# A two-lane decoder kernel on one Trainium2 core: SyncE begins the shifted copies and the expert stores, the queries' norm moves into the exponential's scale, and the lanes' turns change

## What is computed

```python
x = LN(x + state_space(x))           # RMS norm, in-projection, causal convolution, selective scan over T, 16 states
x = LN(x + cross_attention0(x, ctx)) # 16 heads of 64, tanh gate
x = LN(x + experts(x))               # 8 experts, top 2, and one shared expert, FF 512
x = LN(x + window_attention(x))      # 16 heads of 8, rotary, window 128
x = LN(x + cross_attention1(x, ctx)) # 16 heads of 8
x = LN(x + local(x))                 # 2 layers, see below
```

```python
q, k = l2norm(q) * q_scale, l2norm(k) * k_scale
q, k = rotary_xpos(q, k)                       # a query sees its own block of 64 keys and the one before
attn = softmax(mask(8 * q @ k.T)); x = x + (attn @ v) @ wo
h = layernorm(shift(x)) * lg + lb; a, g = split(h @ w1 + b1); x = x + (a * gelu(g)) @ w2 + b2
```

## Time and profile before

| | us |
|---|---|
| median of 3 runs | 1565.3 |
| lowest and highest run | 1559.88, 1567.16 |
| span of the profiled execution, first to last instruction | 1544.1 |
| time of the profiled execution itself | not given |
| busy: PE, DVE, ACT, POOL | 1269.2, 1046.3, 808.2, 395.7 |
| mean granted TensorE clock (1 is full speed) | 0.911 |

### The profile page before, as it was taken

The page is one execution under the profiler, slowest core; times in us unless marked ns, Lnnn a source line. Parts: engine busy times, 40 slices in busy tenths (PEclk is TensorE's granted clock), DMA queues, the critical chain, the costliest instruction groups (busy, mean ns, idle before and its releaser), DMA issues. The chain is left out here.

```text
span 1544.1 us, 23279 instructions
## 1 busy us (share of the span) xinstructions
PE 1269.2 (82%) x8400; PEld 815.4 (53%) x8400; DVE 1046.3 (68%) x2162; ACT 808.2 (52%) x2180; POOL 395.7 (26%) x248
## 2 busy tenths in 40 slices
PE   5767878887998888789775888889689988988986
PEld 4412335884665556456531233579456654655663
DVE  4789976226887787378449998741378879746853
ACT  2466423453764556466627553336276636665663
POOL 0036633412000332032011665360400023202300
PEclk9789978997999989999987888989799999999997
DMA  8300001780000100001010000068400000000000
GB/s 298 123 0 1 0 1 54 254 268 19 2 1 1 35 21 15 1 15 28 2 28 0 1 0 1 1 201 263 130 1 2 1 1 22 22 1 14 22 8 14
DMA packets 42179, 72.21 MB, mean 47 GB/s; under 512 B 3793, under 2 KB 27473, under 8 KB 41810
## 3 DMA queue, kind: packets, MB, share of 16 engines
q1 hardware_dynamic: 28242, 56.30, 10.8%
q10 hardware_dynamic: 11776, 10.23, 2.6%
q0 software_dynamic: 2048, 4.20, 0.9%
HBM read 51.19 MB, written 13.24 MB: 42 GB/s over the span
## 5 line engine op out<-in xcount | busy, mean ns | idle before, releaser
L912 POOL TENSOR_TENSOR scratch<-scratch 128x1024 f32<-128x1024 f32 x64 | 149.7, 2353 | 140.4 <-DVE scratch L883 119.9
L634 POOL TENSOR_TENSOR small<-small,w_const 128x16 f32<-128x16 f32 x32 | 101.1, 3163 | 298.2 <-DVE small L1753 298.2
L731 PE MATMUL psum<-scratch,w_const 128*128 128x512 f32 x256 | 148.8, 713 | 18.5 <-POOL scratch L912 18.4
L883 DVE TENSOR_TENSOR_SCAN scratch<-psum,scratch 128x512 f32<-128x512 f32 x128 | 150.1, 1206 | 9.5 <-ACT psum L804 8.9
L634 POOL TENSOR_TENSOR rstd<-rstd,w_const 128x4 f32<-128x4 f32 x32 | 32.8, 1029 | 432.9 <-DVE rstd L596 430.3
L1706 ACT ACTIVATE scratch<-psum,mx 128x128 f32<-128x128 f32 x256 | 90.0, 376 | 72.7 <-DVE mx L1794 71.5
L804 ACT ACTIVATE psum<-scratch,a_neg 128x512 f32<-128x512 f32 x128 | 87.8, 690 | 61.2 <-DVE scratch L883 52.1
L1374 ACT ACTIVATE scratch<-psum,mx 128x256 f32<-128x256 f32 (+1 forms) x256 | 111.2, 465 | 10.0 <-DVE mx L1410 8.4
L720 PE MATMUL psum<-scratch,cb 96*128 96x512 bf16 x128 | 49.7, 428 | 60.6 <-DVE scratch L875 51.3
L1160 ACT ACTIVATE scratch<-psum,scratch 128x128 f32<-128x128 f32 x240 | 68.3, 368 | 54.7 <-PE psum L1101 54.6
L1541 PE MATMUL psum<-w_local,hT 128*128 128x512 f32 x192 | 91.2, 615 | 6.3 <-ACT hT L1523 5.1
(11 more groups left out here) (266 smaller groups left out, 3199.6 us busy)
## 6 DMA issues: line engine op xcount, KB each, us to landing
expert_weights<-in_expert_weights SPq DMA_DIRECT2D x61, 512.0 KB, 5.1
scratch<-scratch ACTq DMA_DIRECT2D x48, 128.0 KB, 2.3
folded_products<-expert_weights SPq DMA_DIRECT2D x8, 512.0 KB, 3.1
folded<-folded_products SPq DMA_DIRECT2D x8, 512.0 KB, 4.7
w_local<-in_local SPq DMA_DIRECT2D x1, 3122.0 KB
sorted_y<-scratch ACTq DMA_DIRECT2D x12, 256.0 KB, 5.6
scratch<-sorted_x SPq DMA_DIRECT2D x4, 704.0 KB, 6.7
scratch<-in_cross SPq DMA_DIRECT2D x1, 2624.5 KB, 12.9
```

The costliest lines, as they stand in the source:

```text
L634: t.eng.tensor_tensor(v, v, W("const", "neg_half").to_broadcast([P, v.shape[1]]), ALU.pow).then_inc(t.s[done], 1)
L731: ins = pe.matmul(sum_banks[c], ident, t.m.hC[:, 2 * ((n - 1) % 2) + c, :], start=(n == 1), stop=(n == NS))
L883: dve.tensor_tensor_scan(t.m.hs[:, n % 2, c, :], t.ps["dA"], t.m.dBu[n % 2][:, c, :], 0.0, ALU.mult, ALU.add)\
L912: t.eng.tensor_tensor(t.m.hC[:, 2 * (n % 2):2 * (n % 2) + 2, :], t.m.hs[:, n % 2], C, ALU.mult)\
```

## The change

1. **Copies and stores.** The pair of shifted copies and the expert stores are begun by SP, in `row_sync`, and no longer by ACT. SP's loop over the blocks runs four steps longer; the stores stand in it behind the same counts of `block_copied`. The copies wait on SP for `v_freed`.
2. **The queries' norm.** DVE multiplies only the keys by their inverse norm (512 columns instead of 1024). The queries' inverse norm becomes the scale of the exponential, read from SBUF for each head, and DVE multiplies the negative row maxima by it in an added product of 128x4, behind a wait for the maximum's own step.
3. **Masks.** For u = 0 the mask matmul is issued first and the wait for the turned queries' and keys' copies (`a_freed`) comes behind it, in a step of its own.
4. **The table.** All five lists are new. Changes of lane and steps: PE 511 to 732 turns, ACT 435 to 558, DVE 714 to 868, POOL 131 to 126, SP 27 to 68. A local layer has 78 steps on PE instead of 74.

The diff, with the lists cut to the first line of one:

```diff
@@ TURNS @@
 TURNS = {
     "pe": [
-        5, 21, 4, 3, 1, 10, 2, 5, 4, 4, 2, 1, 6, 2, 3, 3, 3, 3, 3, 3, 5, 3, 3, 3, 3, 3, 3, 3, 3, 5, 3, 3, 3, 3,
...
+        5, 34, 4, 1, 1, 4, 2, 3, 1, 1, 3, 1, 4, 1, 1, 1, 3, 3, 3, 3, 3, 3, 3, 3, 5, 2, 1, 1, 2, 2, 1, 1, 2, 3,
...
@@ -1139,13 +1155,6 @@
                 n = min(4, NBK - 4 * g) * P
                 act.activation(t.m.xsT[:, 4 * g * P:4 * g * P + n], t.a.take()[:, 0:n], ACT.Copy).then_inc(t.s["a_freed"], 1)
 
-            def store(g):
-                yield
-                n = min(4 * g + 4, NBK)
-                act.wait_ge(t.s["block_copied"], NBK * t.row + n)
-                act.dma_start(t.m.sorted_y[4 * g * P:n * P, :].rearrange("(b p) d -> p b d", p=P), t.m.xs[:, 4 * g:n, :])\
-                    .then_inc(t.s["sorted_stored"], 16)
-
             yield from take_group(0)
             for b in range(NBK):
                 if b % 4 == 1 and 4 * (b // 4 + 1) < NBK:
@@ -1160,9 +1169,6 @@
                     ins = act.activation(t.m.hid[:, b % 2, f, :], tok(bank, f), ACT.Gelu_apprx_tanh,
                                          bias=t.m.bias[:, f, b:b + 1])
                 ins.then_inc(t.s["a_freed"], 1)
-                if b >= 5 and b % 4 == 1:
-                    yield from store(b // 4 - 1)
-            yield from store(NBK // 4)
 
         def experts_vector(t):
             dve = t.eng
@@ -1572,10 +1578,11 @@
                 q, before = j * P, 64 if j else 0
                 for u in range(2):
                     yield
-                    if u == 0:
-                        pe.wait_ge(t.s["a_freed"], turned_in)
                     r, bank = 64 * u, t.a.open()
                     pe.matmul(bank, cbv["ident"], mask, start=True, stop=False, skip_group_check=True)
+                    if u == 0:
+                        yield
+                        pe.wait_ge(t.s["a_freed"], turned_in)
                     for g in range(4):
                         own = bank[:, g * P:(g + 1) * P]
                         qs, ks = t.m.qT[r:r + 64, j % 2, g, :], t.m.kT[r:r + 64, g, :]
@@ -1673,11 +1680,6 @@
                 if i >= 2:
                     t.w(t.s["vx_loaded"], 32)
                 act.activation(t.m.vv[:, i % 2, :], t.v.take(), ACT.Copy).then_inc(t.s["v_freed"], 1)
-                yield
-                if i >= 1:
-                    act.wait_ge(t.s["v_freed"], t.v.at)
-                    act.dma_start(t.m.vx[0:64, i % 2, :], t.m.vv[64:P, (i - 1) % 2, :]).then_inc(t.s["vx_loaded"], 16)
-                    act.dma_start(t.m.vx[64:P, i % 2, :], t.m.vv[0:64, i % 2, :]).then_inc(t.s["vx_loaded"], 16)
 
             def take_out(j):
                 yield
@@ -1703,8 +1705,9 @@
                     t.w(t.s["max_ready"])
                     for a in range(4):
                         c = 8 * (j % 2) + 4 * u + a
+                        q_root = t.m.small[:, 2 * (j % 2) + 1, 2 * a + u:2 * a + u + 1]
                         ins = act.activation(tok(t.m.pr[:, u, :], a), tok(bank, a), ACT.Exp, bias=t.m.mx2[:, c:c + 1],
-                                             accum_out=t.m.sums2[:, c:c + 1])
+                                             scale=q_root, accum_out=t.m.sums2[:, c:c + 1])
                     ins.then_inc(t.s["a_freed"], 1)
                 yield
                 if j:
@@ -1768,9 +1771,9 @@
                 yield from t.w.step(ins)
                 yield from t.w.step(dve.tensor_tensor(t.m.turned, t.m.turned, t.m.qk[:, i % 2], ALU.add))
                 t.w(t.s["root_ready"])
-                h = lambda v: v.rearrange("p (h d) -> p h d", h=2 * H5)
-                rn = t.m.small[:, 2 * (i % 2) + 1, 0:16].rearrange("p (h o) -> p h o", o=1).to_broadcast([P, 2 * H5, DH5])
-                dve.tensor_tensor(h(t.m.turned), h(t.m.turned), rn, ALU.mult).then_inc(t.s["rope_ready"], 1)
+                k = t.m.turned[:, 512:1024].rearrange("p (h d) -> p h d", h=H5)
+                rn = t.m.small[:, 2 * (i % 2) + 1, 8:16].rearrange("p (h o) -> p h o", o=1).to_broadcast([P, H5, DH5])
+                dve.tensor_tensor(k, k, rn, ALU.mult).then_inc(t.s["rope_ready"], 1)
 
             def add_out(j):
                 yield
@@ -1791,8 +1794,11 @@
                 for u in range(2):
                     yield
                     bank, c = t.a.take(), 8 * (j % 2) + 4 * u
-                    dve.tensor_reduce(t.m.mx2[:, c:c + 4], bank.rearrange("p (a z) -> p a z", a=4), X, ALU.max,
-                                      negate=True).then_inc(t.s["max_ready"], 1)
+                    q_root = t.m.small[:, 2 * (j % 2) + 1, u:8:2]
+                    yield from t.w.step(dve.tensor_reduce(t.m.mx2[:, c:c + 4], bank.rearrange("p (a z) -> p a z", a=4), X,
+                                                          ALU.max, negate=True))
+                    dve.tensor_tensor(t.m.mx2[:, c:c + 4], t.m.mx2[:, c:c + 4], q_root, ALU.mult)\
+                        .then_inc(t.s["max_ready"], 1)
                 scored = t.a.at
                 yield
                 if j + 1 < NT:
@@ -1913,10 +1919,16 @@
             t.w(t.s["scattered"], 16 * 2 * NT)
             for n, (a, z) in enumerate(((0, 4), (4, NBK))):
                 sp.dma_start(m.xs[:, a:z, :], blocked(m.sorted_x[a * P:z * P, :])).then_inc(t.s[f"sorted{n}_loaded"], 16)
-            for k in range(BUFS, NBK):
+            for k in range(BUFS, NBK + BUFS):
                 yield
                 sp.wait_ge(t.s["block_copied"], NBK * t.row + k - BUFS + 1)
-                load(k)
+                if k < NBK:
+                    load(k)
+                done = k - BUFS + 1
+                if done % 4 == 0 or done == NBK:
+                    a = 4 * ((done - 1) // 4)
+                    sp.dma_start(blocked(m.sorted_y[a * P:done * P, :]), m.xs[:, a:done, :])\
+                        .then_inc(t.s["sorted_stored"], 16)
             yield
             t.w(t.s["norm_ready"], 3)
             sp.dma_start(m.folded[:, :], folded_dram[B + b]).then_inc(t.s["score_loaded"], 16)
@@ -1924,7 +1936,18 @@
             t.w(t.s["norm_ready"], 3)
             if t.row < last:
                 sp.dma_start(m.folded[:, :], folded_dram[b + 1]).then_inc(t.s["score_loaded"], 16)
-            else:
+            t.skip(v=NB + 1 + 2 * NS + NT + 3 + 1 + NT + 2 * len(WPAIRS) + NT)
+            for l in range(DEPTH):
+                t.skip(v=1)
+                for i in range(1, NT):
+                    t.skip(v=1)
+                    yield
+                    sp.wait_ge(t.s["v_freed"], t.v.at)
+                    sp.dma_start(m.vx[0:64, i % 2, :], m.vv[64:P, (i - 1) % 2, :]).then_inc(t.s["vx_loaded"], 16)
+                    sp.dma_start(m.vx[64:P, i % 2, :], m.vv[0:64, i % 2, :]).then_inc(t.s["vx_loaded"], 16)
+                    t.skip(v=2 if i == 1 else 3)
+                t.skip(v=4 + 1 + NH)
+            if t.row == last:
                 yield
                 t.w(t.s["y_ready"])
                 sp.dma_start(tokens(out[b]), m.out).then_inc(t.s["stored"], 16)
```

## The result

In the first comparison the changed kernel took 1546.5 us (median of 4 runs) beside 1562.6 for the kernel before: ratio 0.990, interval 0.9866 to 0.9935. Repeated in another session with 12 and 29 runs, it took 1540.4 beside 1542.1: ratio 0.9974, interval 0.9945 to 1.0002. The kernel before took 1562.6 in one session and 1542 to 1546 in the three others, so the second comparison, with more runs, weighs more: there the change is worth 4 us by its ratio and under 2 by the medians, not 16, less than a measurement tells from nothing. Executions of one kernel are further apart than the few tenths of a per cent stated above: the kernel before ran from 1530.1 to 1559.3 us within the second comparison. A ratio leaves out the few executions that stand clearly apart from the rest of their kernel (one of experiment 2's took 2969 us), and need not equal the quotient of the medians.

A forecast was written before the change was run, and what follows sets the result against it. No engine was full on average: VectorE bounds the scans, TensorE the experts and windowed attention, waits the local layers' short parts. Terms -15 - 6 - 5 - 2 + 8 + 9 - 10 = -21 gave 1544 from 1565.3, range 1526 to 1557.

The forecast's parts named there:

- rival (a): Waits only move; masks and issues gain, half the chain's and experts' cost takes 8 back: 1562 us, chance 0.18.
- The 21.2 us around the span: Median 1565.3 less the profile's span 1544.1, taken as time lying around the span, unchanged; the forecast counted from the median.
- Lanes apart: Layer norms of the local layers: the other lane's work covers TensorE's idle time and lower clock, -15 us, at most 29.7.
- the rest of the table: Finer turns on PE and DVE let a ready lane pass a waiting one: -10 us, between 15 slower and 35 faster.
- Eight more table loads: ScalarE in the local layers: 24 loads instead of 16, 10.3 us as the bound, taken as zero on the path.
- Masks: The mask matmul of u = 0 no longer waits for the key copy: -6 us, at most 8.
- Copies by SyncE: ScalarE loses 24 pairs of issues that delay its copy of the queries: -5 us, between 0 and 8.6.
- The halved product: VectorE's product over 512 columns instead of 1024 saves it 19.5 us; taken as -2, from 0 to 5.
- the chain: Maximum, exponential, turn: small products and the scale from a tile add 35.8 us of latency, mostly covered by the other lane: +8.
- rival (c): Slower through the scores' chain between row maximum and probabilities, 35.8 us if nothing covers it: 1582 us, chance 0.14.
- SP's order in the experts: Lane 0's rows issued 7.1 us later per half, 14.2 us, less 5 of weight waits: net +9, bounds 0 and 27.
- The condition for "wrong": Forecast wrong if the local layers stay as long as before, or the experts are longer by over 10 us per half.

The follow-up runs named there:

- experiment 2: Two kernels: all edits of the code with the old turns, ratio 1.0002 to the kernel before; the old code with the new turns, 1.0057.
- three edits undone, experiment 9: Changed kernel with queries' norm on VectorE, masks behind the wait and copies by ScalarE again: 1542.5 us, ratio 0.9975 to the kernel before.
- experiment 6: Changed kernel with the mask of u = 0 issued behind the wait for the turned keys again: 1542.9 us beside the changed kernel's 1540.4.
- experiment 8: Changed kernel with sorted rows first and norm on VectorE (1503.4 us), and to it added either the small product of the maxima (1512.4) or the exponential's scale from a tile (1513.4).
- experiment 1: Changed kernel with lane 0's sorted rows loaded ahead of lane 1's weights on SP, as before the change: 1518.4 us, ratio 0.981 to the kernel before.
- both repairs: Changed kernel with lane 0's sorted rows ahead of lane 1's weights on SP and queries' norm on VectorE: 1503.4 us, ratio 0.9753 to the kernel before.

## Why the prediction was right, and where it was not

The forecast, -21 us to 1544, came out 2 us beside the first median, and that is luck: it was counted from a level of 1565.3 us which the kernel before had in the first session alone, and its sum was too good. By the second comparison the change gives 4 us, what rival (a) had. The forecast was right in what moves, and its sum was off by about 17.

- **The 21.2 us around the span: wrong.** They are 1.8. The difference of the earlier trace rows to the median can only be spread from execution to execution, though the clocks of that first session aren't on record: the kernel before ran from 1535.7 (mean granted clock 0.920) to 1562.6 us (0.903) within one session. The sum, taken from 1565.3, stood on a level that other sessions don't show; a forecast of this kernel can only be one of a difference.
- **Lanes apart (-15) and the rest of the table (-10): about right in the local layers, wrong elsewhere.** With three edits undone, the new turns give 522.5 - 502.6 = 20 us there: TensorE's idle time falls by 11.0 us, and the rest is clock won back, the two parts that the prediction had. It hangs on where the split steps stand, since the old code in the new turns gave 4 us. The finer turns also gave 8.7 us in the first scans, which I had put at nothing, and lost 2.2 and 6.3 in the cross stages ahead of the experts. Why these got longer was not tried.
- **Eight more table loads at no cost: nothing against it.** The loads are 24 of 1.283 us, and TensorE is busy 19.6 of 20 us around some of them. No run tried the term by itself.
- **Masks (-6): not shown.** The wait moved onto the copy of the queries, as said, but no gain could be measured, and experiment 6 speaks against 4 us or more.
- **Copies by SyncE (-5, at most 8.6): mis-sized.** 10 us by medians, 13 by ratios; the 18 of the local layers are half clock. The bound was read from a trace of the old turns; in the new ones the copy of the queries is what TensorE waits for, and 13.5 us of idle time stand at the issues ahead of it.
- **The halved product (-2) and the chain (+8): the step that failed most.** The lengths in the chain were about right: 161 ns for 200, and 467 for 376 + 90. The halved product is not half as long: 687 ns where 1218 / 2 = 609 was taken, so VectorE saves 32 x 0.53 = 17.0 us and not 19.5, and with the small products' 10.2 back only 7. The Trainium skill, ScalarE: Activation LUTs, What ACT_TABLE_LOAD costs, has some 93 ns for each operand from a tile; the trace has 91. But of the latency, 64 x 0.16 + 256 x 0.091 = 33.5 us, 19.4 show by the medians and 22.8 in the local layers, about two thirds, where I took 8 of 35.8 because the other lane should cover most of it. Most of what shows is the longer exponentials' (experiment 8). The likely reason, argued from the waits and not tried by itself: both lanes are in the same part and share ScalarE, so the longer exponentials of one delay the copies of the other. With the norm on VectorE TensorE waits less for ScalarE's copies of the heads (1686, 9.9 to 6.7 us) and of the probabilities (1716, 6.4 to 4.0), not only for the exponentials (1709, 7.4 to 4.5). And the 7 us less for VectorE were worth nothing that shows. This is rival (c)'s mechanism at about two thirds of its price.
- **SP's order in the experts (+9): mis-sized.** 10.4 + 11.9 = 22.3 us. The place was right. The 7.1 us of delay took the second wait from the earlier trace rows, where lane 1's blocks_known came 2.9 us after lane 0's rows; in the changed kernel lane 0 is further ahead of lane 1, and the delay is 11.9 us in the first half and 7.6 in the second (experiment 1). That makes 19.5 us where the sum had 14.2, and the clock, which the term left out, is lower behind the wait. Waits for weights did fall, from 10.8 to 6.4 us, but they are 6.2 with the rows first too, so it is not this order that gives them back. The condition for "wrong", experts longer by over 10 us per half, came true in the first half, not in the second.

With the measured sizes: turns -20 - 8.7 + 8.5, copies -10, chain and product +19, SP's order +22, and -4 to -10 that the new turns give in the experts without it (223.4 us with both repairs, 227.0 and 233.3 before). That is +1 to +7 where -4 was measured; with the copies at the 18 us of the stages it would be -7 to -1. The sizes are not known better than that, and experiment 9 shows that they need not add up.

## What to carry to other kernels

A wait moved on a shared issuing queue costs what the later of the two lanes' events costs on the new schedule, not on the old one; look at what stands behind it, and let loads that feed the next matmul go before weights that don't. Work taken off an engine that nobody waits for is worth nothing, while 91 ns more in each exponential, 23.3 us in all, cost 10 us by the medians and 15.6 in the local layers with both lanes in the same part. When several edits come with a new order, cost each against the new order: the issues, worth 8.6 us at most by the old one, were worth 10 to 13 in it.

## What the runs showed of the hardware

The granted clock is not a function of the program. In 500 to 510 us of the kernel before it was 0.65 in one execution and 1.00 in another, behind the same work, and over the 23 executions of one session the time follows the mean clock: 1535.7 us at 0.920, 1544.8 at 0.911, 1562.6 at 0.903 (roughly: 1541.7 at 0.912 stands beside 1543.3 at 0.918). The Trainium skill says, in TensorE: Matmul & The Clock Gate, What's actually happening, that the window of the activity monitor behind the gate is free-running and isn't reset when a kernel starts, which fits a marginal stretch falling either way. A wait can also cost more than its length: with the rows first (experiment 1) TensorE was idle 9.0 us less in the experts, and they were 22.2 us shorter, at a granted clock of 0.89 and 0.91 instead of 0.84 and 0.83. Differences of a few us between two profiles of this kernel therefore mean nothing unless they are read from stages in which the clock was the same, or beside TensorE's idle time.
